# Causal-attention and soft-MoE block on one core: v sums through a ones matrix, the softmax exchange inside SBUF, two pairs of fold banks

## What is computed

```
q, k, v = mlp_q(x), mlp_k(x), mlp_v(x)        # mlp: gelu(x @ W1 + b1) @ W2 + b2
scores  = (q @ k.T) / scale * tril(ones)       # causal, no softmax
x       = layernorm(x + layernorm(scores @ v) * ln_w + ln_b)
xn      = layernorm(x) * gamma + beta
logits  = unit(xn) * scale @ unit(mu)          # 16 experts x 16 slots = 256 columns
dispatch, combine = softmax(logits, over tokens), softmax(logits, slots)
slot_in  = dispatch.T @ xn ; slot_out = expert mlps(slot_in)
x       = layernorm(x + combine @ slot_out)
```

## Time and profile before

| | |
|---|---|
| median of 3 runs | 605.73 us (604.13 to 606.28) |
| profiled execution | 605.86 us, of which the span is 604.0 us |
| PE busy | 583.9 us, 97% |
| DVE, ACT, POOL busy | 477.7, 393.8, 343.1 us |
| attention block / routing / experts and mixing | about 0 to 406, 407 to 526, 526 to 604 us of the span |

### The profile page before, as it was taken

One profiled execution on the slowest core, in us unless ns is written; L12 is line 12 of the kernel. 1 busy time (PEld: TensorE's weight loads), 2 busy tenths in 40 slices (PEclk: granted clock), 3 DMA queues, 4 the chain that ended last, 5 costly groups with the idle time before them and its releaser, 6 DMA issues. The chain is left out here.

```text
span 604.0 us, 12082 instructions
## 1 busy us (share of the span) xinstructions
PE 583.9 (97%) x3844; PEld 543.3 (90%) x3844; DVE 477.7 (79%) x1012; ACT 393.8 (65%) x888; POOL 343.1 (57%) x359
## 2 busy tenths in 40 slices
PE   7899999999999999999999999989999999999995
PEld 5789999989999998999998999979989898899995
DVE  5869779788797797887978979989777776457776
ACT  4565766676667676667676667567776767426664
POOL 1728558586595585775956857665734342104443
PEclk9989999999999999999999999989999999999998
DMA  8314133142241330422413403205545455723344
GB/s 224 86 69 105 16 91 71 36 105 34 71 104 17 87 77 31 100 35 69 104 17 87 97 10 70 33 7 137 153 128 153 129 153 153 173 76 105 139 141 174
DMA packets 130957, 55.37 MB, mean 92 GB/s; under 512 B 74190, under 2 KB 126828, under 8 KB 130924
## 3 DMA queue, kind: packets, MB, share of 16 engines
q1 hardware_dynamic: 130912, 54.96, 35.7%
q10 hardware_dynamic: 12, 0.00, 0.0%
HBM read 29.78 MB, written 16.78 MB: 77 GB/s over the span
## 5 line engine op out<-in xcount | busy, mean ns | idle before, releaser
L511 POOL TENSOR_TENSOR h_lo<-xn_all,h_hi 128x512 fp32r<-128x512 f32 x32 | 41.3, 1292 | 115.4 <-ACT xn_all L590 115.4
L588 ACT ACTIVATE h_hi<-bank,bias_col 128x512 fp32r<-128x512 f32 x96 | 66.4, 691 | 31.9 <-PE bank L709 28.6
L707 PE MATMUL bank<-xnT_hi,w_hi 128*128 128x512 f32 x188 | 76.1, 405 | 0.0
L708 PE MATMUL bank<-xnT_lo,w_hi 128*128 128x512 f32 x188 | 74.4, 396 | 0.0
L709 PE MATMUL bank<-xnT_hi,w_lo 128*128 128x512 f32 x188 | 74.2, 394 | 0.0
L1492 PE MATMUL bank<-xn_all,e_tok 128*128 128x257 f32 x256 | 65.4, 381 | 1.8 <-ACT slot_inT L1427 1.8
L1080 DVE TENSOR_TENSOR state_lo<-bank,state_hi 128x512 fp32r<-128x512 f32 x57 | 39.2, 688 | 31.8 <-ACT state_hi L625 31.8
L1565 PE MATMUL bank<-w_sb,ET_all 128*128 128x256 f32 x256 | 60.0, 397 | 0.0
L1565 PEld LDWEIGHTS bank<-w_sb,ET_all 128*128 128x128 f32 x256 | 59.8, 329 | 0.0
L625 ACT CAST state_hi<-bank 128x512 fp32r<-128x512 f32 x57 | 33.5, 588 | 37.2 <-PE bank L839 37.2
L1404 ACT ACTIVATE e_tok<-bank,shift,xinv 128x256 f32<-128x256 f32 x64 | 36.2, 566 | 32.7 <-PE bank L1482 26.6
(11 more groups left out here) (188 smaller groups left out, 2054.8 us busy)
## 6 DMA issues: line engine op xcount, KB each, us to landing
x_all<-in_L_attn_x SPq DMA_DIRECT2D x16, 512.0 KB, 3.8
kT<-k_turn SPq DMA_DIRECT2D x128, 64.0 KB, 2.5
e_scratch<-e_turn SPq DMA_DIRECT2D x16, 512.0 KB, 3.2
ET_all<-e_scratch SPq DMA_DIRECT2D x64, 128.0 KB, 2.8
xn_all<-in_xT SPq DMA_DIRECT2D x15, 512.0 KB, 4.5
out<-xn_all SPq DMA_DIRECT2D x15, 512.0 KB, 3.0
w_sb<-in_L_ffn_w SPq DMA_DIRECT2D x2, 512.0 KB, 5.5
xn_all<-in_L_ffn_w SPq DMA_DIRECT2D x2, 512.0 KB, 6.2
```

The costliest lines, as they stand in the source:

```text
L511: pool.tensor_tensor(h_lo[:, V_SLOT, m, :], hv[:, m, :], h_hi[:, V_SLOT, m, :].bitcast(F32), ALU.subtract).then_inc(hv_split, 1)
L588: nc.scalar.activation(h_hi[:, h_slot(j, n), m, :], ps, ACT.Gelu, bias=bias(n, m))
L707: nc.tensor.matmul(ps, w[0], xs[0], start=start, stop=False, skip_group_check=shared)
L708: nc.tensor.matmul(ps, w[0], xs[1], start=False, stop=False, skip_group_check=shared)
```

## The change

1. `carry` becomes two matmuls whose weights are a matrix of ones (`ones_r`) and whose moving operand is, per place in the group, the sum over all earlier tiles of gamma x v (`v_sum`, 128 tokens deep; the ones sum over the partitions). DVE builds the sums tile by tile (`sum_v`, `close_sum`, L1090 and L1099: scalar_tensor_tensor with v_tok and the former v_sum, both in SBUF), ACT rounds them in two halves (`round_vsum`), POOL forms the rest in two halves (`split_vsum`, L530). `preload`, `split_gamma` and the gamma rounding go. `carry` now comes before the end of a chunk's own output and not after its state update, and waits for `vsum_split`.
2. The exchange of e goes from SBUF to SBUF, four DMAs per group with runs of 32 floats, in place of the write to HBM and four reads. `ET_all` is now contiguous for one tile.
3. Fold banks alternate between sequences (`fold_ps(b)`: banks 4, 5 and 6, 7); turning and copying of the slots of sequence b - 1 move to after the second fold of sequence b. The loops over sequences of the MoE block are unrolled.
4. Order: the factors of mu come after v's bias in the first group; ln_b, `scale_tokens`, `norms`, `apply_z`, `invert_z`, `invert_x1` and half of `finish_out` of the last group change places, some into the MoE block. `mark_out` becomes `warm_up` with three banks; `causal` shrinks to one tile. mu shares space with the staged weights.

```diff
-                def carry(a, ba, i):
-                    c = i % GT
-                    if c == 0:
-                        pe.wait_ge(gam_split, a + 1)
-                    if i > 0:
-                        pe.wait_ge(preloaded, PB * ba + i)
-                    split3(out_tile((i + 1) % GT), (gam_hi[:, c:c + 1].to_broadcast([P, P]), ...), ...)
+                def carry(a, c, start):
+                    pe.wait_ge(vsum_split, 2 * a + c // 2 + 1)
+                    nc.tensor.matmul(out_tile(c), ones_r[:, :], vsum_hi[:, c, :], start=start, stop=False,
+                                     skip_group_check=True)
+                    nc.tensor.matmul(out_tile(c), ones_r[:, :], vsum_lo[:, c, :], start=False, stop=False,
+                                     skip_group_check=True)
...
                     elif c == 0:
-                        read_state(ba, i, c, p, False)
+                        read_state(ba, i, c, p, True, False)
+                        carry(a, c, False)
                         last = attend_chunk(a, c, False, True)
                     else:
-                        attend_chunk(a, c, False, False)
-                        last = read_state(ba, i, c, p, True)
+                        attend_chunk(a, c, True, False)
+                        carry(a, c, False)
+                        last = read_state(ba, i, c, p, False, True)
                     last.then_inc(chunk_done, 1)
                     if i < TB - 1:
                         update_state(a, c, i == 0)
-                        carry(a, ba, i)
...
+                def sum_v(g, j, c):
+                    dve.wait_ge(v_biased, 2 * g + c // 2 + 1)
+                    if not (isinstance(g, int) and g == 0):
+                        dve.wait_ge(v_summed, GT * g + c)
+                        dve.wait_ge(vsum_split, 2 * g)
...
+                        last = nc.vector.scalar_tensor_tensor(out=v_sum[:, c + 1, :], in0=v_tok[:, c, :], scalar=gamma,
+                                                              in1=v_sum[:, c, :], op0=ALU.mult, op1=ALU.add)
+                    last.then_inc(v_summed, 2 if j == GB - 1 and c == GT - 2 else 1)
...
+                def split_vsum(g, m):
+                    pool.wait_ge(vsum_rounded, 2 * g + m + 1)
...
+                    if attend and project:
+                        split_vsum(a, 0)
                     if project:
                         split_hv(g, 0)
                     if attend:
                         invert_o(pool, a, 0)
                     if project:
+                        if attend:
+                            split_vsum(a, 1)
                         split_hv(g, 1)
...
-                    sp.dma_start(e_scratch[g].rearrange("f p n -> p f n"),
-                                 e_turn[g % 2][:, :, :, :].rearrange("p f c t -> p f (c t)")).then_inc(e_stored, 16)
-                    sp.wait_ge(e_stored, 16 * g + 16)
...
+                    for j in range(FOUR):
+                        quad = slice(QUAD * j, QUAD * j + QUAD)
+                        sp.dma_start(ET_all[:, g, :, quad],
+                                     e_turn[g % 2][quad, :, :, :, :].rearrange("r f s t c -> r (f s t c)")
+                                     ).then_inc(e_moved[g % 2], 16)
...
-                    if t == 0:
-                        pe.wait_ge(slot_inT_ready, SB * b + SB)
+                    if t == 0 and b > 1:
+                        pe.wait_ge(slot_inT_ready, SB * b)
...
                         fold(b, t)
+                        if t == 1 and b > 0:
+                            turn_slots(b - 1)
...
-                            last = nc.tensor.matmul(mix_ps[k % 2][t][:, 0:D], group[:, t, :],
+                            last = nc.tensor.matmul(mix_ps[k % 2][t][:, 0:D], ET_all[:, k, GT * s + t, :],
                                                     so[:, k // GB, s, :], start=(s == 0), stop=(s == SB - 1))
```

More of the change, by code:

```diff
@@ L524, in split_v @@
                                        ALU.subtract).then_inc(v_split, 1)
+                def split_vsum(g, m):
+                    pool.wait_ge(vsum_rounded, 2 * g + m + 1)
+                    pair = slice(2 * m, 2 * m + 2)
+                    pool.tensor_tensor(vsum_lo[:, pair, :], v_sum[:, pair, :], vsum_hi[:, pair, :].bitcast(F32),
+                                       ALU.subtract).then_inc(vsum_split, 1)
                 def invert_mu_norms():
@@ L546, in body @@
                             invert_mu_norms()
-                        add_ln_b(g)
+                        if attend and more:
+                            add_ln_b(g)
                         if not more:
@@ L550, in body @@
                         split_ktok(g, 0)
+                        if not more:
+                            split_v(g, 0)
                     if attend:
@@ L684, in body @@
                         follow(2)
-                        if settle:
+                        if settle and more:
                             apply_z(act, a - 1, (ja - 1) % 2, range(GT))
+                        if not more:
+                            norms(act, 0, 0, range(GT))
                         follow(3)
@@ L1160, in body @@
                     turn_k(g, 3)
-                    if not more:
-                        dve.wait_ge(hv_split, 2 * GROUPS)
-                        scale_tokens(1, 1)
                     if attend:
@@ L1176, in body @@
                     if attend:
+                        if not more:
+                            sum_v(g, j, 0)
                         add_out(dve, a, 2)
                         add_out(dve, a, 3)
+                        if not more:
+                            return
                         z_summed(dve, a, 1)
-                    split_gamma(g)
+                    sum_v(g, j, 0)
                     if attend:
@@ L1421, in route @@
                         step(b, t, last)
+                        if first and GT <= t < 2 * GT:
+                            apply_z(act, GROUPS - 2, 0, (t - GT,))
                         if first and t >= TB - GT:
@@ L1433, in _ @@
                 route(0, last=False, first=True)
-                with act.Fori(1, B - 1) as b:
+                for b in range(1, B - 1):
                     route(b, last=False)
@@ L1518, in _ @@
                 pe.wait_ge(ones_set, GB)
-                with pe.Fori(0, B - 1) as b:
+                for b in range(0, B - 1):
                     route(b, last=False)
```

241 lines of the change are left out of this document (133 added, 108 removed).

## The result

The changed kernel takes 611.9 us (median of 4 runs, 611.3 to 612.04) where the kernel before took 605.45 (604.13 to 606.28): ratio 1.0118, 95% interval 1.0091 to 1.0145. It is slower, by 6.5 us; the forecast was 611.0.

The account below looks back on a forecast made before the run. PE was taken as the bound, busy 583.9 of 604.0 us. Terms -7.0 + 18.2 + 3.0 - 3.9 + 1.5 - 2.3 + 0 - 4.3 = +5.2 on 605.86 gave 611.0 us, range 604 to 617.

Parts of the forecast that it names:

- PE passes: Attention carries: two matmuls instead of three, 60 carries either way, sixty matmuls less at 0.117 us each: -7.0 us.
- The new wait: Chunk 0 of 11 groups: PE waits for POOL's first half of vsum_lo, 1.65 us each, at least 0.85: +18.2 us.
- later chain: POOL at the seam: held by DVE's sum, second v_lo, var_z, r_z and r_all come later: 0.45 us per group.
- lost race: One of two DVE sums behind masked_lo goes just before POOL turns to vsum_lo, delaying it: 0.35 us in the sum.
- hold works one way: Rival: DVE does not hold POOL, so PE waits 0.85 to 0.95 us per group; 602 us, chance 0.20.
- First groups of a sequence: Three groups without carry in chunk 0: later masked_lo, sums and q split delay PE 1.0 us each: +3.0 us.
- First group: Start of kernel: PE's 2.3 us wait for b2T goes, and 1.6 us of halved clock behind it: -3.9 us.
- End of attention: Last group and passage into MoE block: one wait shrinks, moved and added work costs more: +1.5 us, least certain term.
- first rival: First in the rivals' list: DVE does not hold POOL; its sign was vsum_lo waits of 0.9 us each; chance 0.20.
- Routing: Seams between sequences: three PE waits of 0.6 us and 0.2 of slower restart each are covered: -2.3 us.
- exchange: SBUF-to-SBUF DMAs of e in 128-byte runs keep pace with routing, 6.3 against 7.2 us a group: 0, up to +3.
- mixing: Contiguous weights load in 189 ns instead of 329, saving 17 ns per instruction over 256: -4.3 us.

Follow-up runs that it names:

- vsum_early: Changed kernel with POOL's first half of vsum_lo moved ahead of invert_x1, behind invert_z, at the end of the body before: 601.21 us, ratio 0.9947 to before.
- one_input: Changed kernel whose v sums read one SBUF tensor, not two, leaving out the sum over earlier tiles: ratio 1.0090 to before.
- moe_part: Attention block of the kernel before, with the changed kernel's exchange, ET_all, fold banks and unrolled loops: 596.49 us, ratio 0.9877 to before.
- before_pad64: Kernel before with 64 unused bytes per partition ahead of h_hi, nothing else: ratio 1.0025 to before.

## Why the prediction was right, and where it was not

The total came out within 1 us, and the side too, but the closeness is luck: the wait and the way out of attention were each far off, in opposite directions.

- **PE passes, -7.0.** Right: a middle group has four matmuls less, 0.47 us, and each second matmul with ones is 0.12 behind the first.
- **The new wait, +18.2.** The mechanism and place are right, and vsum_early proves them. The step that failed is the size: 1.65 us per group, of which 0.45 for a later chain and 0.35 for a lost race. The chain to `r_all` is not later, counted from the start of the group: the pair of `v_lo` grew by 0.18, and `project_v`, 0.14 longer in each group, moves the start from which it is counted later too. The race at the end went as I feared, POOL began `vsum_lo` 0.18 behind the first sum, but it took only 0.15 longer; it was DVE that waited (1.89 us for two sums). The gap is 0.93, close above the floor of 0.85, and 0.1 more is lost behind it: 11 x 1.02 = 11.2. So for the size the rival "hold works one way" was nearest, and as a mechanism it was wrong: one_input shows both ways. From one row, 0.2 us on one `ktok_lo` (0.26 against the 1.19 that `ktok_lo` takes elsewhere in that trace), I took DVE to hold POOL for the whole length of a sum. POOL waits only for what is left of the sum when it begins: the second `v_lo` began with 0.32 left and took 0.17 more.
- **First groups of a sequence, +3.0.** Wrong: no new wait there. These three groups got shorter, by 0.5, 0.5 and 1.3 us: each has three carries of two passes where it had four of three, 0.7 us less, and the waits for `masked_lo` are gone. Of the 1.3, 0.8 belongs to the execution that was profiled: its wait of 1.0 for `masked_lo` stands in one group only, and moe_part, with the same attention code, takes 24.06 us there and not 24.89.
- **Not in the sum at all: slower projections, +2.9.** No row of before could give it; the prediction took it for granted that an unedited matmul costs the same. It does not when its operands move.
- **First group, -3.9.** The wait for `b2T` and the window at 0.50 are gone, as said. But the 1.6 for the clock is not a gain of every execution: before_pad64 has the same wait of 2.3, and its clock stays at 1.00 behind it. The text named the mu row as "what is late next" and priced it at nothing: it is 1.2 us. Two more waits of 0.5 (for `kT` and `state_lo`) follow, and the longer warm-up (L792 with six matmuls for L772 with four) starts the first hidden layer 0.9 later. Left: -0.9.
- **End of attention, +1.5 (-3 to +4).** Wrong, and outside its own bounds: +6.8. The parts were listed, but as if each lay beside PE. What failed is that the DVE work sent into the MoE block was counted and not laid along DVE's queue: from 414.9 on it is busy for 17 us with hardly a gap, and all exps wait behind it. By my estimate from the two windows at 0.85 and 0.73, about 1.5 of the 6.8 is the clock after the wait. And before had such a loss of its own just there, which the profile happened to catch: its clock stands at 0.84 and 0.59 from 394 to 400, and before_pad64, with the same code, is at 1.00 there and takes 13.5 us for the passage to the logits, not 15.3. So the change's real price here is nearer 8.5: the two rows of the table together take 44.6 us, and 36.2 in before_pad64 and 36.3 in moe_part. How much of it each moved step costs is not shown.

```profile
394.00:397.00 3.00, 1.64 (x10) 1.67 (x11) 2.88 (x8) 2.96 (x10) 2.56 (x4) 0.84 0.02 5
397.00:400.00 3.00, 3.00 (x18) 3.00 (x17) 1.90 (x7) 2.01 (x5) 3.00 (x3) 0.59 0.00 0
```

- **Routing, -2.3, exchange, 0, mixing, -4.3.** -2.6, nothing, and -4.4, and moe_part confirms them apart from the rest. Of the two statements of the Trainium skill that the prediction set against each other, the one that limits the penalty on small descriptors to HBM (DMA: Bandwidth & Descriptors, Why small descriptors are slow) is the one that the forecast went by, and the cost of nothing came true: 128 KB in 128-byte runs landed in 3.8 us, and PE waits for none. That such runs carry no penalty is not shown: the 512 KB loads of `x_all` from HBM landed in the same 3.8 us.
- **Signs asked for.** `vsum_lo` in PE's waits: yes, twelve times 0.8 and not eleven times 1.6, which by the prediction's own list is the first rival's row. `v_sum` above 0.48 on average (829 ns) and `vsum_lo` above 1.28 (1369): yes. `b2T`, the clock, the seams, 190 ns: yes.

So the sum was right through errors that cancel. By the stages of the table they are +3.0 (first group), -6.8 (attention), +5.3 (end of attention), -0.3 and -0.1 (routing and mixing), which add to +1.1: 6.3 measured where 5.2 was forecast. Within attention it is -7.0 for the size of the wait, -3.0 for the first groups and +2.6 for the projections; most of the rest is seven of the sixty carry matmuls saved, 0.8 us, which the table books here and which fall in the first and the last group.

## What to carry to other kernels

When a change adds a small instruction on a third engine that PE needs early, look for its earliest legal slot: here ten of the microseconds hung on whether it stood before or after four steps that nobody was waiting for. Work moved across a stage boundary must be laid along the queue of the engine that takes it, there and then; an engine 80% busy on average was full for the 17 us in which it mattered, and shifting single steps only renamed the wait. And compare unedited instructions too, before and after: new tensors move the old ones.

## What the runs showed of the hardware that was not expected

- The place of a matmul's operands in SBUF changes its pace: 24 matmuls of `project_v` take 2.72 to 2.88 us, and 12 of `project_k` 1.435 to 1.47, with shifts of `h_hi` and what lies behind it by 64 to 11264 bytes. Group for group, the same addresses give the same times in every kernel; but with the same operands three groups of before take 2.83 where the others take 2.72. The rule is open.
- DVE and POOL hold each other both ways, the later one until the earlier is through: a 128x256 sum with two SBUF inputs that begins during POOL's half ends 0.28 us behind it (0.48 us alone, up to 1.38 here), and POOL's half is longer by what is left of the sum, less some 0.15 (0.29 left, 0.13 more; 0.40 left, 0.24 more). A 128x256 `tensor_scalar` with one SBUF input is held as well, 698 ns on average against 344, and ends 0.15 behind POOL.
- After waits of 1.7 to 3.4 us PE's clock was sometimes granted at 0.50 to 0.85 for some microseconds and sometimes not: before and before_pad64 have the same code and the same waits, within 0.2 us, both at 2.3 us in the first group and at 1.8 near the end of attention, and only the first lost its clock behind them. One profile of before can hold such a loss, and it must not be booked to the change.
